# Attention's opening: the weights staged in five column pieces between the parts of the first step

## What is computed

```python
xn = layernorm(x)
proj = xn @ W_in.T                       # x' 512 | z 512 | B 256 | C 256 | dt_low 16
dt = softplus(dt_low @ dt_W.T + dt_b)    # 16 heads
y = scan(x', B, C, dt, A_log) + x' * D_param      # chunks of 64 tokens, state 16 x 32 a head
attn = (y / rms(y) * norm_w * silu(z)) @ W_out.T
logits = xn @ Wc + bc + tie              # 128 columns: 32 experts x 4 sets
perm = logits == max(logits over the 32 tokens of a group)
ffn = gather by perm, two small matmuls per expert, scatter back
out = x + attn + ffn
```

## Time and profile before

| what | value |
|---|---|
| median of 3 runs | 3028.83 us (3025.64 to 3034.0) |
| the profiled execution | 3038.94 us |
| its span in the profile | 3036.7 us |
| mean granted TensorE clock | 0.988 |
| PE busy | 2889.0 us (95%), 59304 matmuls |
| DVE, ACT, POOL busy | 2056.6 (68%), 1697.8 (56%), 1426.6 us (47%) |

### The profile page before, as it was taken

How to read it: one execution, slowest core, us unless ns; L and a number is a source line. 1 busy time by engine, 2 the same in 40 slices (tenths; PEclk the granted TensorE clock), 3 DMA queues, 4 the chain that set the end, 5 groups by cost and what they waited for, 6 DMA issues and landing times.

```text
span 3036.7 us, 134102 instructions
## 1 busy us (share of the span) xinstructions
PE 2889.0 (95%) x59304; PEld 2466.2 (81%) x59304; DVE 2056.6 (68%) x2980; ACT 1697.8 (56%) x3678; POOL 1426.6 (47%) x2287
## 2 busy tenths in 40 slices
PE   7999999999999999999999999997777778999999
PEld 5888888888888888888888888885666667888887
DVE  5777777777777777777777777674444447777775
ACT  5566665666656666566665666653333323555555
POOL 3666666666666667676666766662000001000000
PEclk9999999999999999999999999998999999999999
DMA  4222222222222222222222222216344436877765
GB/s 144 69 80 70 80 74 72 81 70 80 74 78 76 70 80 74 78 75 70 79 74 77 76 74 76 74 40 248 111 127 109 113 100 199 232 217 229 225 203 156
DMA packets 365218, 328.93 MB, mean 108 GB/s; under 512 B 56400, under 2 KB 278096, under 8 KB 363744
## 3 DMA queue, kind: packets, MB, share of 16 engines
q1 hardware_dynamic: 363712, 320.15, 35.5%
q10 hardware_dynamic: 928, 0.20, 0.0%
HBM read 206.96 MB, written 113.31 MB: 105 GB/s over the span
## 4 chain that ended last, share of the span: by engine, by line
PE 90%; DVE 4%; issue 4%; POOL 1%; DMA 1%; ACT 0%; SPq 0%; POOLq 0%; DVEq 0%; ACTq 0%
PE a_proj L920 40%; PE a_mix L920 12%; PE s_rt L1589 8%; PE g_pick_ps L1335 5%; PE a_scan L1031 5%; PE s_w_ps L1559 4%; PE s_rt L1602 4%; DVE g_picked L1302 3%; PE a_scan L1008 3%; PE g_acc_ps L1356 2%; PE a_scan L995 2%; PE a_mix L983 2%; PE a_misc L976 1%; PE a_misc L1049 1%; PE a_misc L1039 0%
## 5 line engine op out<-in xcount | busy, mean ns | idle before, releaser
L920 PE MATMUL a_proj<-wdh,xTh 128*128 128x512 f32 x1024 | 420.9, 411 | 6.2 <-ACT raw L586 5.6
L1525 ACT COPY s_res<-s_rt 128x512 f32<-128x512 f32 x512 | 262.9, 600 | 278.6 <-PE s_rt L1589 278.6
L920 PE MATMUL a_proj<-wdh,xTl 128*128 128x512 f32 x1024 | 403.0, 394 | 2.5 <-issue 2.5
L920 PE MATMUL a_proj<-wdl,xTh 128*128 128x512 f32 x1024 | 402.0, 393 | 0.0
L1538 DVE TENSOR_TENSOR s_resT<-s_w_ps,s_b 128x1024 f32<-128x1024 f32 x252 | 296.7, 1218 | 140.7 <-PE s_w_ps L1559 140.7
L766 DVE COPY_PREDICATED scan_in<-mask,a_scan 64x512 f32<-64x512 uint32 x512 | 379.4, 741 | 16.0
L444 POOL TENSOR_TENSOR dx<-xs,d_row 64x512 f32<-64x512 f32 x256 | 330.8, 1292 | 15.1
L622 ACT ACTIVATE scan_in<-CT,hsel 64x128 f32<-64x128 f32 x1024 | 326.1, 388 | 4.8
L452 POOL TENSOR_TENSOR yv<-yt,dx 128x512 f32<-128x512 f32 x128 | 188.9, 1476 | 294.2 <-DVE yt L806 294.2
L1302 DVE COPY g_picked<-g_pick_ps 128x1024 f32<-128x1024 f32 x128 | 156.7, 1224 | 230.3 <-PE g_pick_ps L1335 230.3
L586 ACT ACTIVATE raw<-a_proj,rs 128x272 f32<-128x272 f32 x128 | 62.3, 488 | 428.2 <-PE a_proj L920 428.2
(11 more groups left out here) (138 smaller groups left out, 7294.2 us busy)
## 6 DMA issues: line engine op xcount, KB each, us to landing
x<-in_x_dram SPq DMA_DIRECT2D x128, 256.0 KB, 2.6
xn_dram<-xn SPq DMA_DIRECT2D x128, 256.0 KB, 2.4
part_dram<-res SPq DMA_DIRECT2D x128, 256.0 KB, 2.6
g_xn<-xn_dram SPq DMA_DIRECT2D x128, 256.0 KB, 2.9
s_w<-in_w_dram SPq DMA_DIRECT2D x128, 256.0 KB, 3.9
s_part<-part_dram SPq DMA_DIRECT2D x128, 256.0 KB, 3.6
out_dram<-s_out SPq DMA_DIRECT2D x128, 256.0 KB, 2.9
xr<-in_xT_dram SPq DMA_DIRECT2D x126, 256.0 KB, 2.8
```

The costliest lines, as they stand in the source:

```text
L920: last = nc.tensor.matmul(out, lhs[a], rhs[c], start=(k == 0 and n == 0), stop=(k == nk - 1 and n == 2))
L1525: nc.scalar.copy(res[:, n % 4, :, :], rt_bank[:, n % 3, :, :]).then_inc(res_cp, 1)
```

## The change

The pieces become column blocks over all four row blocks: 0 = B (256 columns), 1 = x (512), 2 = z (512), 3 = C and logits (384), 4 = W_out. Each has means, centring, rounding and rest of its own, and these stand between the parts of step 0 rather than ahead of it. Piece 3 overlaps the place of xT(2) and W_out that of pieces 0 and 3, so SP waits for `w_lo` of 4 before W_out and xT(2). The x copies `xs` are placed in another order, so that piece 2 keeps its place while xs 0 is written. The statistics of tiles 0 and 1 move behind B's rest, and those of tile 2 behind z's rest.

```diff
-    stage = [sb(f"stage{i}", [P, 2, KI * D], at=a) for i, a in enumerate((AT_W1, AT_ONEHOT))]
+    stage = [sb(f"stage{i}", [P, KD, c], at=a) for i, (a, c) in enumerate(
+        ((AT_W1, C_DT), (AT_ONEHOT, DI), (AT_ONEHOT + 8192, DI), (AT_W1 + 4096, TCOLS - C_C), (AT_W1, D)))]
...
-    xs = [[sb(f"xs{c}_{j}", [P, H, HD], at=AT_ONEHOT + 2048 * (4 * c + j)) for j in range(4)] for c in range(2)]
+    xs = [[sb(f"xs{c}_{j}", [P, H, HD], at=AT_ONEHOT + 2048 * (2 * j + c)) for j in range(4)] for c in range(2)]
...
+    stages = [(io["w_tok"][:, :, 0:C_DT], [w[:, :, C_B:C_DT] for w in wt]),
+              (io["w_dz"][:, :, 0:DI], [w[:, :, 0:DI] for w in wd]),
+              (io["w_dz"][:, :, DI:2 * DI], [w[:, :, DI:2 * DI] for w in wd]),
+              (io["w_tok"][:, :, C_DT:], [w[:, :, C_C:TCOLS] for w in wt]),
+              (io["w_out"], [w[:, :, :] for w in wo])]
```

SP:

```diff
+        load_weights(0)
+        for i in range(2):
+            load_xr(0, i)
         for t in range(2):
             load_x(t)
-        for n in range(LAST_STAGE):
-            sync.dma_start(stage_view(n), stages[n][0]).then_inc(w_in[n], 16)
-            if n == 1:
-                for i in range(2):
-                    load_xr(0, i)
+        load_weights(1)
+        for dst, name in rows:
+            sync.dma_start(dst[:], io[name].partition_broadcast(P)).then_inc(const_in, 16)
         for dst, name in consts[6:]:
             sync.dma_start(dst[:], io[name]).then_inc(const_in, 16)
-        for dst, name in rows:
-            sync.dma_start(dst[:], io[name].partition_broadcast(P)).then_inc(const_in, 16)
+        load_weights(2)
         load_x(2)
-        gather["load_small"](sync)
-        sync.wait_ge(w_lo, 1)
-        sync.dma_start(stage_view(LAST_STAGE), stages[LAST_STAGE][0]).then_inc(w_in[LAST_STAGE], 16)
-        sync.wait_ge(w_lo, 2)
+        load_weights(3)
         for i in range(2):
             load_xr(1, i)
+        gather["load_small"](sync)
         for t in range(2):
             store_xn(t, t)
+        sync.wait_ge(w_lo, LAST_STAGE)
+        load_weights(LAST_STAGE)
...
                 sync.wait_ge(xT_lo, s + 1)
+                if s == 0:
+                    sync.wait_ge(w_lo, LAST_STAGE)
                 load_xr(s + 2, 0)
```

ACT:

```diff
-        for n in range(LAST_STAGE):
-            stage_hi(n)
-            if n == KD // 2 - 1:
-                hi_x(0)
-        for t in range(2):
-            normalize(t)
-        act.wait_ge(const_in, NCONST)
-        nc.scalar.activation(a_row[:], a_row[:], ACT.Exp).then_inc(a_ready, 1)
-        gather["cast_ident"](act)
+        hi_x(0)
+        stage_hi(0)
...
                 copy_bdt(n0 + 1)
+            if s == 0:
+                stage_hi(1)
+                for t in range(2):
+                    normalize(t)
+                act.wait_ge(const_in, NCONST)
+                nc.scalar.activation(a_row[:], a_row[:], ACT.Exp).then_inc(a_ready, 1)
             if valid(s + 1):
                 hi_x(s + 1)
...
+            if s == 0:
+                stage_hi(2)
             if valid(s):
                 copy_x(n0)
...
             if s == 0:
-                stage_hi(LAST_STAGE)
+                stage_hi(3)
+                gather["cast_ident"](act)
...
             if valid(s - 1):
                 square(n1, 0)
+            if s == 0:
+                stage_hi(LAST_STAGE)
```

DVE (`centre` and `stage_lo` now take one piece n whole):

```diff
-        for t in range(2):
-            stats(t)
-            finish_stats(t)
         for n in range(LAST_STAGE):
-            if n % 2 == 0:
-                centre(n)
-                centre(n + 1)
+            centre(n)
+            if n == 0:
+                lo_x(0)
             stage_lo(n)
-            if n == KD // 2 - 1:
+            if n == 0:
                 dve.wait_ge(wdt_hi, 1)
                 nc.vector.tensor_tensor(wt[1][:, :, C_DT:C_C], misc[:, 0:KD * H].rearrange("p (k h) -> p k h", k=KD),
                                         wt[0][:, :, C_DT:C_C].bitcast(F32), ALU.subtract).then_inc(wdt_lo, 1)
-                lo_x(0)
+                for t in range(2):
+                    stats(t)
+                    finish_stats(t)
+            if n == 2:
+                stats(2)
+                finish_stats(2)
...
                 lo_x(s + 1)
-                stats(2 * (s + 1))
-                finish_stats(2 * (s + 1))
+                if s > 0:
+                    stats(2 * (s + 1))
+                    finish_stats(2 * (s + 1))
```

PE (`column_means` now takes one piece n; `project_x(0)`, `project_z(0)`, `project_c(0)` wait for `w_lo` of 2, 3, 4):

```diff
-        for n in range(0, LAST_STAGE, 2):
-            column_means(n)
-        pe.wait_ge(const_in, NCONST)
-        pe.wait_ge(w_lo, KD // 2)
+        column_means(0)
+        pe.wait_ge(w_lo, 1)
         pe.wait_ge(wdt_lo, 1)
         pe.wait_ge(zeroed, 8)
         for s in range(NST + 2):
...
                 project_bdt(n0)
                 project_bdt(n0 + 1)
+            if s == 0:
+                column_means(1)
+                column_means(2)
             if valid(s - 1):
                 transpose_b(n1)
             if valid(s):
                 project_x(n0)
+            if s == 0:
+                column_means(3)
+                pe.wait_ge(const_in, NCONST)
```

More of the change, by code:

```diff
@@ L561, in stage_hi @@
                 act.wait_ge(centred, n + 1)
-            for rawp, hi, lo in stage_parts(n):
-                if n == LAST_STAGE:
-                    for k in range(KI):
-                        last = nc.scalar.activation(hi[:, k, :], rawp[:, k, :], ACT.Copy, scale=nwcol[:, k:k + 1])
-                else:
-                    last = nc.scalar.copy(hi, rawp)
+            hi = stages[n][1][0]
+            if n == LAST_STAGE:
+                for k in range(KI):
+                    last = nc.scalar.activation(hi[:, k, :], stage[n][:, k, :], ACT.Copy, scale=nwcol[:, k:k + 1])
+            else:
+                last = nc.scalar.copy(hi, stage[n][:])
             last.then_inc(w_hi, 1)
@@ L704, in stage_lo @@
             dve.wait_ge(w_hi, n + 1)
-            for rawp, hi, lo_ in stage_parts(n):
-                if n == LAST_STAGE:
-                    for k in range(KI):
-                        last = nc.vector.scalar_tensor_tensor(lo_[:, k, :], rawp[:, k, :], nwcol[:, k:k + 1], hi[:, k, :].bitcast(F32),
-                                                              ALU.mult, ALU.subtract)
-                else:
-                    last = nc.vector.tensor_tensor(lo_, rawp, hi.bitcast(F32), ALU.subtract)
+            hi, lo_ = stages[n][1]
+            if n == LAST_STAGE:
+                for k in range(KI):
+                    last = nc.vector.scalar_tensor_tensor(lo_[:, k, :], stage[n][:, k, :], nwcol[:, k:k + 1], hi[:, k, :].bitcast(F32),
+                                                          ALU.mult, ALU.subtract)
+            else:
+                last = nc.vector.tensor_tensor(lo_, stage[n][:], hi.bitcast(F32), ALU.subtract)
             last.then_inc(w_lo, 1)
@@ L736, in centre @@
         def centre(n):
-            dve.wait_ge(mean_ps, 1 + n // 2)
-            view, banks = stage_view(n), scan_bank[:, n // 2 * 2:n // 2 * 2 + 2, :].rearrange("p b c -> p (b c)")
-            cols = view.shape[2]
-            for c0 in range(0, cols, 512):
-                c1 = min(c0 + 512, cols)
-                last = nc.vector.tensor_tensor(view[:, :, c0:c1], view[:, :, c0:c1],
-                                               banks[:, c0:c1].unsqueeze(1).to_broadcast([P, 2, c1 - c0]), ALU.subtract)
-            last.then_inc(centred, 1)
+            dve.wait_ge(mean_ps, n + 1)
+            cols = stage[n].shape[2]
+            nc.vector.tensor_tensor(stage[n][:], stage[n][:], scan_bank[:, n, 0:cols].unsqueeze(1).to_broadcast([P, KD, cols]),
+                                    ALU.subtract).then_inc(centred, 1)
         def expand_c(n):
@@ L940, in project_x @@
             if n == 0:
[L941 removed]
+                pe.wait_ge(w_lo, 2)
             if n % 2 == 0:
@@ L948, in project_z @@
         def project_z(n):
+            if n == 0:
+                pe.wait_ge(w_lo, 3)
             if n % 2 == 0:
@@ L1053, in column_means @@
         def column_means(n):
-            view = [stage_view(n + i) for i in range(2)]
-            cols = view[0].shape[2]
+            cols = stage[n].shape[2]
             pe.wait_ge(zeroed, 5)
-            for i in range(2):
-                pe.wait_ge(w_in[n + i], 16)
-            for b, c0 in enumerate(range(0, cols, 512)):
-                c1 = min(c0 + 512, cols)
-                for k in range(KD):
-                    last = nc.tensor.matmul(scan_bank[:, n + b, 0:c1 - c0], mean[:], view[k // 2][:, k % 2, c0:c1],
-                                            start=(k == 0), stop=(k == KD - 1))
+            pe.wait_ge(w_in[n], 16)
+            for k in range(KD):
+                last = nc.tensor.matmul(scan_bank[:, n, 0:cols], mean[:], stage[n][:, k, :], start=(k == 0), stop=(k == KD - 1))
             last.then_inc(mean_ps, 1)
```

22 lines of the change are left out of this document (4 added, 18 removed).

## The result

The changed kernel is slower. Its median is 3045.4 us (3042.31 to 3050.5, 6 runs) against 3031.93 us of the kernel before in the same runs (3025.64 to 3036.04). The ratio is 1.0046, interval 1.0033 to 1.0058, which is +14 us (10 to 18). The forecast was +10.1 us, and 3038.9 for the time. Of the 6.5 us between 3038.9 and 3045.4, 3.1 are that the kernel before was itself over the earlier median here (3031.93 against 3028.83); the other 3.4 are the size of the change, whose forecast lies at the lower edge of the measured interval. The profiled execution took 3043.23 us.

A forecast was written before the change was run, and what follows sets the result against it. TensorE (PE) was taken as the bound, 90% of the chain that ended last. New waits moved tile 3's B/dt projection from 57.4 to 67.5, +10.1 us on the median 3028.83, giving 3038.9 us; range 3031 to 3046.

The forecast's parts named there:

- the mark: Start of token tile 3's B/dt projection on PE in step 1 (second step): forecast 67.5 us against 57.4, +10.1.
- start of the first projection: PE's first projection of B and dt in the opening: forecast at 20.0 us, 5.9 earlier than in the kernel before.
- first new wait (zeros): PE waits for POOL's eight zeroings, behind inv_std of tiles 0 and 1: 5.3 us, from 14.6 to 19.9.
- projections of B and dt: 24 PE products of 272 columns after the opening's idle time, costed at 1.2 GHz: 5.4 us, to 25.4.
- sums: PE's sums after tile 2's softplus: forecast at 46.7 us against 43.58, with PE waiting 1.6 us for them.
- T: The end of the rest of C's weights in the opening: forecast at 50.6 us.
- The queue: SP's loads: x tile 3 issued at about 52.9 us behind W_out, xT(2) and the rs stores, landing at 57.2.
- rival A: Tile 3 doesn't queue up but lands beside W_out, at 55.5: +8.4 us, 3037.2; chance 0.18.
- Rival F: PE's clock is low after 67.5 and the next 5.65 us run at half: up to +2.8, 3041.7; chance 0.15.
- from there on nothing in the diff runs: Behind tile 3's B/dt projection no changed code runs, and the stages of step 1 hang from its start.
- rival B: The pipeline's fill takes the delay up, 2.2 us idle in 55.8 to 82: +7.9, 3036.7; chance 0.08.
- a difference in the steady part: Sign against the prediction: the steady part was costed at zero, only the x tiles' places in memory changing.

The follow-up runs named there:

- zeros_first: The changed kernel with POOL's three memsets of zeros ahead of inv_std of tiles 0 and 1; ratio to the kernel before 1.003.
- x3_first: The changed kernel with x tile 3 issued right behind the wait for w_lo = 4, ahead of W_out and xT(2); ratio to the kernel before 1.0036.
- after_again: The changed kernel, nothing altered, run and profiled once more; ratio to the kernel before 1.0049.
- x3_early: The changed kernel with x tile 3 loaded ahead of the loop, right behind x tile 2; ratio to the kernel before 1.0037.
- x3_early_picks: The changed kernel with x tile 3 loaded ahead of the loop and DVE making picks(0) before W_out's rest; ratio to the kernel before 1.0027.
- xs_order: The kernel before with only the new order of the xs places in memory; ratio to the kernel before 1.0001.
- shift_pe: The kernel before with already-met waits on PE, making its program 4 instructions longer, no work or order changed; ratio to the kernel before 0.9996.
- shift_others: The kernel before with 16 already-met waits each on ACT and DVE, PE's program as before; ratio to the kernel before 0.9991.

## Why the prediction was right

The chain stood to within 1 us at every step up to the mark, in part by errors that cancelled. Behind the mark the agreement is in part luck.

- The start of the first projection was 20.93, not 20.0. Half of it is DVE's first operation, which came 0.5 later (dt's weights), and B's means took 3.78 instead of 3.4. The first new wait (zeros) was 5.4 us by the rows of after (15.32 to 20.68) for the 5.3 charged; zeros_first moved the first projection by 6.1 and the mark by 5.0.
- The projections of B and dt were charged 5.4 us at 1.2 GHz for all 24 products. They took 4.4 (20.93 to 25.35). Their starts were 0.227 us apart for 12 products and 0.125 from then on, so the full clock was back 3 us after PE resumed. This term was forecast too large by 1.0 and the start too early by 0.9; these cancelled, and x's projection came at 35.64 for 35.8.
- z's projection (42.20 for 42.4), sums (46.58 for 46.7), T (50.46 for 50.6), C's projection (50.89 for 51.1): as worked out.
- The queue: tile 3 was issued at 53.18 (52.9), landed in 4.3 us, at 57.5 (57.2). x3_first shows that 1.5 of it is the queue. The rule on ring order in the Trainium skill, "DMA: Bandwidth & Descriptors", section "Queues, rings and completion order", spoke for a landing behind the bytes ahead, and the trace agrees: 57.5, not the 55.5 of rival A. Nothing of those four loads landed out of order here (W_out at 55.5, xT(2) by 56.9, tile 3 at 57.5).
- The copy of C ended at 61.26 (61.0), W_out's rest started at 64.32 (64.2), lg at 66.98 (67.0), the mark at 67.45 (67.5).
- Rival F was half true. In after the clock was still 1.00 in the gap before the logits, fell as PE resumed, and was half for most of the logits and tile 2's projection; PE's next wait, for lg, hid that. The part that was to cost time, a low clock behind the mark, came in after_again (behind dA, 1.4 us) and not in after. Windows of after: length, busy of PE, PEld, DVE, ACT, POOL, granted clock, DMA share, GB/s.

```profile
60.00:61.30 1.30, 0.00 (x0) 0.00 (x0) 0.00 (x0) 1.27 (x4) 0.00 (x0) 1.00 0.63 225
61.30:64.00 2.70, 2.69 (x13) 2.69 (x14) 0.00 (x0) 2.70 (x5) 0.00 (x0) 0.53 0.31 98
64.00:66.00 2.00, 2.00 (x13) 1.82 (x12) 1.68 (x3) 0.29 (x1) 0.00 (x0) 0.79 0.00 0
```

The step that was weak is the last: "from there on nothing in the diff runs". I equated the shift of one mark with the shift of the end. The first pair of profiles has +10.1 at the mark and +8.7 at picks(2); the second +11.1 and +12.8. The rows say what lies between. PE's wait for dA grew from 2.2 to 2.7 us in both pairs, so nothing was taken up there, and rival B (the fill absorbs) is not shown by any run. The 1.4 us less of the first pair are two stalls without a releaser in before's profile (0.7 and 0.9) that after's lacks. The 1.7 more of the second pair are mainly the clock behind dA. In x3_early, x3_early_picks and zeros_first, gains at the mark were spent in the same two ways, mostly on the clock, and in x3_early_picks on a longer wait for dA as well.

The yardstick itself was one profile. With the openings of xs_order, shift_pe and shift_others counted too, the mark of the old opening lies between 55.13 and 57.38, so that the forecast took the latest of five; from their mean the two marks of the changed kernel are 11 to 12 us later. The +14 (10 to 18) agrees with the 10.7 and 11.6 us at the sums of step 1 and with 8.7 to 12.8 at picks(2). Whether the 1 to 5 us above that are noise or belong to the steady part stays open: by the profiles it is 2 to 10 us longer in the changed kernels, by the times shift_pe shows none of it. The prediction named a difference in the steady part as a sign that it would be wrong, so costing that part at zero is not confirmed.

One slip in the sums: the range's upper end, 3041.7 with 5 for the spread and 0.9 for a late first piece, is 3047.6, not 3046. The measured 3045.4 lies below both, close to the end.

## What to carry to other kernels

When a load or a preparation step is moved, list for each engine's queue what now stands behind the new wait, and follow the first thing on the list to where another engine waits for it: here a 256 KB tile behind 1.5 MB in the queue (3.5 us at the mark), W_out's rest ahead of picks(0) (2.0) and three memsets (5.0) made up the loss at the mark. Splitting a preparation in pieces pays only if each piece's work is issued when it lands, ahead of the work that doesn't need it; with its means behind the projections the change gained nothing even without its three new waits, and with x's means ahead, beside some smaller moves, it won 0.29%. And a gain at one mark of a pipeline's fill is not a gain of the time: read it again two steps later, with the granted clock behind every wait, and in more than one profile.

## What was not expected of the hardware

- The granted clock's column says 1.00 from 20.5 to 23.7 us in after, while the products there stand 0.227 us apart for 272 columns, which is 1.2 GHz (windows of after, columns as above, and two pairs of rows of PE's timeline):

```profile
20.50:23.70 3.20, 2.77 (x12) 2.80 (x13) 0.00 (x0) 0.00 (x0) 0.18 (x2) 1.00 0.09 28
```

```profile
22.20 0.43 PE L914 MATMUL a_proj<-wth,xTl 128*128 128x272 f32 x1
22.43 0.43 PE L914 MATMUL a_proj<-wth,xTh 128*128 128x272 f32 x1
24.34 0.29 PE L914 MATMUL a_proj<-wtl,xTh 128*128 128x272 f32 x1
24.47 0.29 PE L914 MATMUL a_proj<-wth,xTl 128*128 128x272 f32 x1
```

  In this stretch the distance of products tells the clock, and the column doesn't. In zeros_first the column reads 0.50 from 14 to 20 us already, so it isn't always silent at the start.
- The clock can be half behind a PE wait of 2.7 us in one run and full in the next run of the same program (after_again and after), and full or half behind a wait of 2.2 (before 1.00; xs_order 0.50 from 68.0 to 71.3 us).
- Some 13 steps take longer than the others (11, 13, 15, 26, 28, 30 and so on), the same in every kernel, with 8.3 to 14.1 us of PE idle time without a releaser in sum and the falls of the clock behind it. A step takes 31.27 or 31.31 us, the same in two profiles of one kernel and different between kernels. What sets either isn't shown here, beyond that four instructions more in PE's program went with two more of the long stalls.
